# A two-layer graph-attention kernel on one core: keys loaded in four parts, guard scores from step 2, mask rows in 32 pieces, one turn of row maxima, and an output projection in 16-bit halves

## The reference, cut to what matters

```python
# layer 0: h = relu(layernorm(x)); x = x + gat(h, adj)          (8 heads, 4096 nodes, 512 features)
# layer 1: h = relu(layernorm(x))
keys    = einsum('nj,hjk->hnk', h, Wks)      # 8 heads of 64
queries = einsum('nj,hjk->hnk', h, Wqs)
values  = einsum('nj,hjk->hnk', h, Wvs)
adj     = maximum(adj, eye(n))
atts    = einsum('hqk,hmk->hqm', queries, keys) / 64 ** 0.5
atts    = softmax(atts - 1e+16 * (1.0 - adj)[None], axis=-1)
x       = x + einsum('hqm,hmk,hko->qo', atts, values, Wo)
```

## Time and profile before

| | us |
|---|---|
| median of 3 runs | 5021.12 |
| lowest and highest run | 5012.5, 5022.32 |
| the profiled execution, own time | 5012.62 |
| its span, first to last instruction | 5010.9 |
| TensorE matmul busy | 4584.9 (91%) |
| VectorE busy | 3379.6 (67%) |
| ScalarE busy | 3110.1 (62%) |
| GpSimd busy | 3452.4 (69%) |
| mean granted TensorE clock | 0.965 |

### The profile page before, as it was taken

The page is one execution under the profiler, slowest core; times in us unless marked ns, Lnnn a source line. Parts: engine busy times, 40 slices in busy tenths (PEclk is TensorE's granted clock), DMA queues, the critical chain, the costliest instruction groups (busy, mean ns, idle before and its releaser), DMA issues.

```text
span 5010.9 us, 128860 instructions
## 1 busy us (share of the span) xinstructions
PE 4584.9 (91%) x43282; PEld 2220.7 (44%) x43793; DVE 3379.6 (67%) x6969; ACT 3110.1 (62%) x5768; POOL 3452.4 (69%) x2969
## 2 busy tenths in 40 slices
PE   5679999999999878699999899999999999999998
PEld 2322222222222234245555555555555555555555
DVE  6868888888888633556656556557557557466565
ACT  3345555555555333167777677677687687677675
POOL 1157776676777500078878788788788788788786
PEclk8789999999999989789999999999999999999999
DMA  7743233233232234453523425325244334334334
GB/s 310 311 115 97 87 109 93 91 111 93 92 108 70 92 100 118 149 131 91 150 74 110 131 73 139 99 77 156 78 109 134 86 101 135 93 98 130 92 100 120
DMA packets 354936, 583.29 MB, mean 116 GB/s; under 512 B 31200, under 2 KB 219648, under 8 KB 337088
## 3 DMA queue, kind: packets, MB, share of 16 engines
q1 hardware_dynamic: 348992, 557.63, 37.4%
q0 software_dynamic: 5120, 16.78, 1.1%
q10 hardware_dynamic: 128, 0.13, 0.0%
HBM read 497.61 MB, written 76.82 MB: 115 GB/s over the span
## 4 chain that ended last, share of the span: by engine, by line
PE 37%; issue 4%; DMA 3%; SPq 3%; DVE 2%; ACT 1%; POOL 1%; DVEq 0%; ACTq 0%; POOLq 0%
PE d_gd L1475 9%; PE d_sc L1490 6%; PE d_sc L1491 6%; PE d_sc L1492 5%; PE d_acc L1509 3%; PE d_acc L1511 3%; PE d_acc L1519 3%; DMA d_KA<-scratch_kl 3%; PE d_misc L1534 2%; POOL d_PL L1264 1%; SPq L1152 1%; DVE d_junk L1359 1%; ACT d_PH L1305 1%; ACT d_PF L1301 1%; SPq L1153 1%
## 5 line engine op out<-in xcount | busy, mean ns | idle before, releaser
L1264 POOL TENSOR_TENSOR d_PL<-d_PF,d_PH 128x512 f16<-128x512 f32 x2048 | 2357.0, 1176 | 630.6 <-ACT d_PH L1305 628.3
L1359 DVE CUSTOM_DVE_ANT_0 d_junk<-d_gd,d_MR 128x512 bf16<-128x512 f32 x2112 | 1445.0, 690 | 779.2 <-PE d_gd L1475 712.2
L1301 ACT ACTIVATE d_PF<-d_sc 128x512 f32<-128x512 f32 x2048 | 1234.0, 603 | 767.4 <-remote 385.1
L709 DVE SCALAR_TENSOR_TENSOR b_P<-b_R,u,b_A 128x512 f32<-128x512 f32 x1792 | 1202.4, 743 | 217.8 <-ACT b_A L621 154.8
L1305 ACT ACTIVATE d_PH<-d_sc 128x512 f16<-128x512 f32 x2048 | 1239.6, 605 | 0.0
L750 PE MATMUL b_acc<-b_P,V 128*64 128x512 f32 x4096 | 943.2, 601 | 38.1 <-DVE b_P L709 25.3
L1475 PE MATMUL d_gd<-d_KA,d_QA 128*128 128x512 f16 x2112 | 817.7, 387 | 135.6 <-DVE d_gm L1359 47.5
L1490 PE MATMUL d_sc<-d_QA,d_KA 128*128 128x512 f16 x2048 | 783.6, 383 | 64.9 <-ACT d_PH L1305 37.3
L1491 PE MATMUL d_sc<-d_QL,d_KB 128*128 128x512 f16 x2048 | 781.8, 382 | 0.0
L1511 PE MATMUL d_acc<-d_V,d_PH 128*128 128x64 f16 x8192 | 643.4, 194 | 0.0
L1509 PE MATMUL d_acc<-d_V,d_PH 128*128 128x65 f16 x8192 | 642.4, 193 | 0.1
(11 more groups left out here) (128 smaller groups left out, 3916.5 us busy)
## 6 DMA issues: line engine op xcount, KB each, us to landing
d_stage<-in_adj SPq DMA_DIRECT2D x144, 512.0 KB, 4.3
d_V<-scratch_v SPq DMA_DIRECT2D x131, 520.0 KB, 4.3
a_rows<-in_adj SPq DMA_DIRECT2D x32, 2048.0 KB, 9.5
b_stage<-in_adjT SPq DMA_DIRECT2D x128, 512.0 KB, 3.6
d_MT<-scratch_mt SPq DMA_DIRECT2D x36, 1024.0 KB, 6.3
d_KA<-scratch_kh SPq DMA_DIRECT2D x66, 512.0 KB, 8.1
d_KA<-scratch_kl SPq DMA_DIRECT2D x66, 512.0 KB, 10.2
d_KB<-scratch_kh SPq DMA_DIRECT2D x264, 128.0 KB, 3.0
```

The lines of the kernel that those rows point to most:

```text
L709: nc.vector.scalar_tensor_tensor(out=PT[:, m % P_STEPS, h, :], in0=R[:, par, h, :], scalar=T["u"][:, m, h:h + 1], in1=A[m % A_RING][:, :], ...
L1264: eng.tensor_tensor(PL[:, t % H_RING, :], PF[:, t % F_RING, :], PH[:, t % H_RING, :], ALU.subtract).then_inc(s_lowp if by_pool(t) else s_l ...
L1301: nc.scalar.activation(PF[:, t % F_RING, :], sc[t % 2][:, :], ACT.Exp, scale=EXP_SCALE)
L1359: nc.vector.tensor_tensor_reduce(out=junk[:, gi % 2, :], in0=gd[gi % 2][:, :], in1=MR[:, s, c * QB:(c + 1) * QB], scale=1.0, scalar=-3.0e3 ...
```

## The change

In the layer-1 attention:
- `load_ka` loads a quarter of the keys (four loads of 128 KB). It is called at mb = 7, 15, 23 and 31, ahead of `load_kb`, and for the pair *after* the next, into the buffer that the current pair just finished reading. The keys of the first two pairs are loaded before the loop. `load_q` stays at mb = 0.
- Guards run from step 2 instead of 5. A step then has two or three of them, 64 over 27 steps instead of 24.
- The last quarter of the mask tiles is loaded at step 10 of the next block instead of at mb = 31.
- `mask_chunk` works on 32 chunks of 512 columns, from a ring of six, at most steps from 76 to 114.
- `crow` makes the rows of both heads at once: four small matmuls of two rows instead of eight of one. The copy takes two partitions and multiplies by a selector `only`, so that each head keeps its own row.
- wo and oN are kept as high and low 16-bit halves. `project_out` has twelve 16-bit matmuls instead of four 32-bit ones, `copy_turned` two vector instructions instead of one. The halves of wo are made once, before the loop.

```diff
-    CW = 1024
+    CW = 512
-    FIRST_G, LAST_G = 5, 28
+    FIRST_G, LAST_G = 2, 28
+    MT_LATE = 10
-    S_RING = 3
+    S_RING = 6
-    CHUNK_STEPS = [FIRST_C + 5 * ci // 2 for ci in range(CHUNKS)]
+    CHUNK_STEPS = [FIRST_C + 5 * ci // 4 for ci in range(CHUNKS)]
...
-        def load_ka(sp, par, hp):
+        def load_ka(sp, par, hp, i):
+            cols = slice(i * PER * P, (i + 1) * PER * P)
             for x in range(2):
                 row = (2 * hp + x) * D
-                sp.dma_start(KA[0:D, par, x, :], DR["kh"][row:row + D, :]).then_inc(s_KA[par][x], 16)
-                sp.dma_start(KA[D:P, par, x, :], DR["kl"][row:row + D, :]).then_inc(s_KA[par][x], 16)
+                sp.dma_start(KA[0:D, par, x, cols], DR["kh"][row:row + D, cols]).then_inc(s_KA[par][i], 16)
+                sp.dma_start(KA[D:P, par, x, cols], DR["kl"][row:row + D, cols]).then_inc(s_KA[par][i], 16)
...
                             load_q(sp, par, nxt, nb if hp < HP - 1 else (nb + 1) % NB)
-                            load_ka(sp, par, nxt)
                         if mb % PER == PER - 1:
 
                             sp.wait_ge(s_S, nb * TILES + (hp * PAIR + 2 * (mb + 1) + CREDIT))
+                            load_ka(sp, hp % 2, (hp + 2) % HP, mb // PER)
                             load_kb(sp, nxt, mb // PER)
-                            if hp == HP - 1:
+                            if hp == HP - 1 and mb < NT - 1:
                                 load_mt(sp, (nb + 1) % NB, mb // PER)
+                        if step == MT_LATE and not first:
+                            load_mt(sp, nb, GROUPS - 1)
...
             act.wait_ge(s_const, 16 * 2)
-            act.wait_ge(s_set, 5)
+            act.wait_ge(s_set, 6)
+            nc.scalar.activation(woS[:, 0, :, :], xr[:, :, :], ACT.Copy, scale=W_SCALE).then_inc(s_set, 1)
...
+            dve.wait_ge(s_set, 7)
+            nc.vector.scalar_tensor_tensor(out=woS[:, 1, :, :], in0=xr[:, :, :], scalar=W_SCALE, in1=woS[:, 0, :, :],
+                                           op0=ALU.mult, op1=ALU.subtract).then_inc(s_set, 1)
...
-                for x in range(2):
-                    dve.wait_ge(s_crow, it * 2 + (x + 1))
-                    nc.vector.tensor_scalar(QL[D:D + 1, par, x, :], gd[x][D:D + 1, :], shift[D:D + 1, :], None,
-                                            ALU.add).then_inc(s_crowc, 1)
+                dve.wait_ge(s_crow, it + 1)
+                for x in range(2):
+                    nc.vector.tensor_scalar(QL[D:D + 2, par, x, :], gd[0][D:D + 2, :], shift[D:D + 2, :], only[D:D + 2, x:x + 1],
+                                            ALU.add, ALU.mult).then_inc(s_crowc, 1)
...
-                nc.vector.tensor_copy(oN[:, hp, :], misc1[:, :]).then_inc(s_m1, 1)
+                nc.vector.tensor_scalar(oN[:, 0, hp, :], misc1[:, :], O_SCALE, None, ALU.mult).then_inc(s_oNh, 1)
+                dve.wait_ge(s_oNh, nb * HP + (hp + 1))
+                nc.vector.scalar_tensor_tensor(out=oN[:, 1, hp, :], in0=misc1[:, :], scalar=O_SCALE, in1=oN[:, 0, hp, :],
+                                               op0=ALU.mult, op1=ALU.subtract).then_inc(s_m1, 1)
...
                 s, x, c = gi // (2 * MC), gi // MC % 2, gi % MC
-                if s == 0 and c == 0:
-                    if x == 0:
-                        pe.wait_ge(s_Q[par], count * 96 + 96)
-                    pe.wait_ge(s_KA[par][x], count * 32 + 32)
+                if gi == 0:
+                    pe.wait_ge(s_Q[par], count * 96 + 96)
+                if s == 0 and x == 0 and c % (MC // GROUPS) == 0:
+                    pe.wait_ge(s_KA[par][c // (MC // GROUPS)], count * 64 + 64)
...
                 for s in range(SUB):
-                    mm = nc.tensor.matmul(gd[x][D:D + 1, s * P:(s + 1) * P], cmh[:, x, s:s + 1], idh[:, :], start=True, stop=True,
+                    mm = nc.tensor.matmul(gd[0][D:D + 2, s * P:(s + 1) * P], cmh[:, s, :], idh[:, :], start=True, stop=True,
                                           tile_position=(0, D))
...
                 for c in range(HP):
-                    mm = nc.tensor.matmul(misc1[:, :], oN[:, c, s * P:(s + 1) * P], wo[:, c, :],
-                                          start=(c == 0), stop=(c == HP - 1))
+                    for a, b in TERMS:
+                        mm = nc.tensor.matmul(misc1[:, :], oN[:, a, c, s * P:(s + 1) * P], woS[:, b, c, :],
+                                              start=(c == 0 and a == b == 0), stop=(c == HP - 1 and a == 1))
```

More of the change, by code:

```diff
@@ L1032, in layer1_attention @@
     MASK_OPS = 2 + SUB * ROW_OPS
-    FIRST_G, LAST_G = 5, 28
+    FIRST_G, LAST_G = 2, 28
     CROW_STEP = 30
-    S_RING = 3
+    MT_LATE = 10
+    S_RING = 6
     K = D + 1
+    O_SCALE = 16.0
     COPY_STEP, NORM_STEP, TURN_STEP, BACK_STEP, WO_STEP, STORE_STEP = LAG, 3, 5, 7, 11, 28
@@ L1088, in layer1_attention @@
         PL = sb("d_PL", [P, H_RING, QB], F16)
-        oN = sb("d_oN", [P, HP, QB])
-        wo = sb("d_wo", [P, HP, F])
+        oN = sb("d_oN", [P, 2, HP, QB], F16)
+        woS = sb("d_woS", [P, 2, HP, F], F16)
         xr = sb("d_xr", [P, SUB, F])
@@ L1097, in layer1_attention @@
         cm = sb("d_cm", [P, 2, SUB])
-        cmh = sb("d_cmh", [P, 2, SUB], F16)
+        cmh = sb("d_cmh", [P, SUB, 2], F16)
         shift = sb("d_shift", [P, 1])
+        only = sb("d_only", [P, 2])
         idh = sb("d_idh", [P, P], F16)
@@ L1110, in layer1_attention @@
         s_set = sem("constants_set")
-        s_KA = [[sem(f"ka_in{i}{x}") for x in range(2)] for i in range(2)]
+        s_oNh = sem("normalised_high")
+        s_KA = [[sem(f"ka_in{par}{i}") for i in range(GROUPS)] for par in range(2)]
         s_Q = [sem(f"q_in{i}") for i in range(2)]
@@ L1191, in _ @@
                 load_chunk(sp, 0, ci)
-            load_ka(sp, 0, 0)
             load_q(sp, 0, 0, 0)
+            for i in range(GROUPS):
+                load_ka(sp, 0, 0, i)
             for ci in range(S_RING, CHUNKS):
@@ L1197, in _ @@
                 load_chunk(sp, 0, ci)
+            for i in range(GROUPS):
+                load_ka(sp, 1, 1, i)
             for i in range(GROUPS):
@@ L1252, in _ @@
             for par in range(2):
-                for x in range(2):
-                    sp.wait_ge(s_KA[par][x], 32 * (2 * NB + 1 - par))
+                for i in range(GROUPS):
+                    sp.wait_ge(s_KA[par][i], 64 * (2 * NB + 1))
                 sp.wait_ge(s_Q[par], 96 * (2 * NB + 1 - par))
@@ L1258, in _ @@
                 sp.wait_ge(s_V[i], 16 * (HP * NB + (1 if i < GROUPS - 1 else 0)))
-                sp.wait_ge(s_MT[i], 16 * (NB + 1))
+                sp.wait_ge(s_MT[i], 16 * (NB + (1 if i < GROUPS - 1 else 0)))
         def split(eng, engine, nb, t):
@@ L1396, in add_rows @@
                 dve.wait_ge(s_m1w, nb * M1_USES + (HP + s + 2))
-                nc.vector.tensor_tensor(xr[:, s, :], misc1[:, :], xr[:, s, :], ALU.add).then_inc(s_m1, 1)
+                nc.vector.scalar_tensor_tensor(out=xr[:, s, :], in0=misc1[:, :], scalar=1.0 / (O_SCALE * W_SCALE),
+                                               in1=xr[:, s, :], op0=ALU.mult, op1=ALU.add).then_inc(s_m1, 1)
             def finish(nb, hp, mb):
@@ L1414, in _ @@
                 mask_chunk(0, 0, ci)
-                for gi in range(4 * (ci - CH), 4 * (ci - CH) + 4):
+                for gi in range(2 * (ci - CH), 2 * (ci - CH) + 2):
                     if gi >= 0:
                         guard(0, gi, 2 + ROW_OPS * (gi // (2 * MC) + 1) if gi % (2 * MC) == 0 else None)
-            for gi in range(4 * (CHUNKS - CH), GUARDS):
+            for gi in range(2 * (CHUNKS - CH), GUARDS):
                 guard(0, gi, MASK_OPS if gi % (2 * MC) == 0 else None)
@@ L1445, in body @@
                             mask_setup(nb + 1, (nb + 1) % NB)
-                        if step in CHUNK_STEPS:
-                            mask_chunk(nb + 1, (nb + 1) % NB, CHUNK_STEPS.index(step))
+                        for ci in range(CHUNKS):
+                            if step == CHUNK_STEPS[ci]:
+                                mask_chunk(nb + 1, (nb + 1) % NB, ci)
             body(0, True)
@@ L1460, in _ @@
             pe.wait_ge(s_const, 16 * 2)
-            pe.wait_ge(s_set, 5)
+            pe.wait_ge(s_set, 6)
+            pe.wait_ge(s_set, 8)
             pe.sem_inc(s_S, CREDIT)
@@ L1548, in _ @@
                 guard(0, 0, gi, 0)
-            for x in range(2):
-                crow(0, x)
+            crow(0)
             def body(nb, first):
@@ L1558, in body @@
                             pe.wait_ge(s_Q[hp % 2], count * 96 + 96)
-                            for x in range(2):
-                                pe.wait_ge(s_KA[hp % 2][x], count * 32 + 32)
+                            for i in range(GROUPS):
+                                pe.wait_ge(s_KA[hp % 2][i], count * 64 + 64)
                             pe.wait_ge(s_crowc, nb * (2 * HP) + (2 * hp + 2))
@@ L1575, in body @@
                         if mb == CROW_STEP:
```

(3 more changed lines are left out.)

11 lines of the change are left out of this document (6 added, 5 removed).

## The result

| | before | after |
|---|---|---|
| median, us | 5020.63 | 5086.59 |
| lowest, highest | 5012.5, 5022.32 | 5077.2, 5087.38 |
| span of the profiled execution | 5010.9 | 5084.7 |
| mean granted TensorE clock | 0.965 | 0.953 |

What follows compares the result with a forecast made beforehand. TensorE's order of work was taken to bound the layer-1 attention loop. Terms of - 3.7 - 3 - 1.1 - 6.2 + 25 + 1 gave + 12.0 us a block, + 96 in eight, + 3 before the loop; forecast 5116 us, range 5045 to 5165.

Steps and rivals of the forecast that it cites:

- The idling for the queries: TensorE at guard 0 of each pair start, waiting for late query loads: 17.4 us a block, before the clock's loss.
- The queries' wait, within a block: TensorE at guard 0 of the pair starts inside a block: idling of 3.7, 3.7 and 4.7 us.
- The clock: TensorE behind each query wait: clock falls to 1.2 GHz, losing 1.9 us a gap, 7.6 a block.
- The rival that it stays up: TensorE's clock stays at 2.4 GHz behind gaps of 3.7 us, so 60 us go: 5056 us; chance 0.20.
- The jump: TensorE behind the block jump: guard 0 idles for the queries, 4.0 us at one jump, taken as 5.3.
- VectorE: Sixteen more mask pieces and a second copy instruction in the loop: + 1 us a block, between - 5.9 and + 6.
- 0.7 us a pair for the whole spread: Guards over 27 steps fill TensorE's holes in steps 2 to 4: saves about 3 us a block.
- Projection: Output projection on TensorE: twelve 16-bit matmuls save 0.93 us a row group, 3.7 a block.
- The turn of maxima: Small matmuls on TensorE, four instead of eight: saves 0.27 us a turn, 1.1 a block.
- The keys' wait: TensorE's waits for keys vanish with keys loaded a pair ahead: 6.2 us a block saved, clock included.
- the faster rival: SyncE's issues cost under about 0.25 us, so queries come in time: 4912 us; chance 0.08.
- The lock on the shared port: VectorE's 16 added mask pieces each wait for GpSimd again: 0.41 us each, or up to 0.75.

Runs made afterwards that it cites:

- experiment 1: The changed kernel with the six query loads issued ahead of the four key loads; 4913.74 us, ratio to before 0.9787.
- experiment 2: The changed kernel with guards from step 5 instead of 2; 4943.73 us, ratio to before 0.9844.
- experiment 3: The changed kernel with 16 useless 512-column matmuls on TensorE ahead of guard 0's wait for the queries; 5038.11 us, ratio to before 1.0038.
- Experiment 6: The changed kernel with the last quarter of the mask tiles loaded at mb = 31 again, ahead of the block jump; 5112.98 us, ratio to before 1.0186.
- experiment 5: The changed kernel with query loads ahead of key loads and the mask rows in 16 pieces of 1024 columns; 4913.07 us, ratio to before 0.9793.
- experiment 10: The changed kernel with query loads first, guards from step 3 and 16 mask pieces of 1024 columns; 4905.99 us, ratio to before 0.9792.
- experiment 8: The changed kernel with query loads first and guards from step 3; 4904.25 us, ratio to before 0.9774.
- experiment 7: The kernel before with only the output projection in 16-bit halves, including two instructions in copy_turned; 4997.54 us, ratio to before 0.9957.
- experiment 4: The changed kernel with the mask rows in 16 pieces of 1024 columns and a ring of three again; 5063.86 us, ratio to before 1.0087.
- experiment 9: Query loads first, guards from step 3, plus the last quarter of KA and KB loaded behind the block jump; 4903.51 us, ratio to before 0.9787.

## Why the prediction was right, and which terms were mis-sized

The sign and its cause were right, and the size came out within the range in part by luck, since errors offset each other. The idling for the queries is the example. The forecast's terms make 139 us in eight blocks, and 135.3 were measured. But behind the six jumps it was 12.4 where the terms make 31.8, and at the other 26 pair starts 122.9 where they make 107.4; the sum in the prediction counted eight jumps, and there are six. The first two blocks have none ahead of them. By the end of block 1 the changed kernel was 24 us behind (forecast 15), nearly half of it by the end of the first wait, of 9.3 us; block 2 added 12, as forecast; the six blocks behind a jump added 6.5 each instead of 12. Step by step:

- **The queries' wait, within a block: right.** Forecast 3.7, 3.7 and 4.7 us of idling; the pair starts of one block show 3.86, 4.46 and 5.55, and blocks 3 to 7 on average 3.9, 4.5 and 5.1. Steps 2 and 3 of these three pairs grew by 20.5 us a block, where idling and clock were forecast at 17.8. The last query issue came 7.1 us behind the first issue, as worked out. Experiments 1 and 2 take the wait away by two independent ways and give back 173 and 143 us.
- **The clock: right.** I charged 1.9 us a gap, 60 in all. Filling the gaps gave 48 net, and the mean clocks put the whole at about 70 (experiment 3). The rival that it stays up fell: 0.50 behind the gap.
- **The jump: wrong.** The term "I take 5.3" for the wait behind the block jump measured 1.5 to 3.1, mean 2.1. I took the mask-tile load out of the sum with its issue time of 1.35 us alone. Experiment 6 put it back and got 5.15 us of waiting and 26 us of run time. With its clock term the forecast was 7.2 us a jump, and steps 2 and 3 there grew by 2.9: 26 us too much in six jumps. The next error is of the same size; block 1 and the starts of the other pairs, which cost more than forecast, offset part of both.
- **VectorE: wrong in sign.** I took + 1 us a block. From the step lengths, what waits for VectorE in pairs 3 and 4 (steps 6 to 29, against the same steps of pair 2) went from 5.3 us a block to 2.8, so the term is - 2.5, within the - 5.9 to + 6 that I allowed. The extra work was there (8.2 us a block for pieces, 2.8 for the copy) but hidden (experiments 5 and 10); what I left out is that guards over 27 steps instead of 24 ease VectorE as much as TensorE. Experiments 2 and 8 bear it out: from step 5 to step 3 is worth 39 us, where 0.7 us a pair for the whole spread makes 22, and step 8, where the copy is felt, falls from 3.28 to 2.68 in pairs 1 to 3. Their other difference, the place of the query loads, adds no wait in either. The size of the pieces matters less: with guards from 5 the same steps lose 3.7 us a block with small pieces (experiment 2) and 4.6 with large ones (experiment 7); with guards from 2 it is 2.8 with small and 2.4 with large ones (experiment 4).
- **TensorE's own way over the jump: not in the forecast.** Step 0 behind a jump went from 7.3 to 8.5 us (blocks 3 to 7). The cause stays open (experiment 9).
- **Projection: right on TensorE** (0.92 us less for a row group, forecast 0.93), with a cost on VectorE in the old spread that the new spread hides (experiment 7).
- **The turn of maxima:** step 30 fell from 3.06 to 2.84 us, 0.22 against 0.27.
- **The keys' wait:** gone, as said. Steps 5 and 6, where it stood, are 6.2 us a block shorter, though each step 5 has a guard more; forecast was 6.2.
- **Issue time, the faster rival:** refuted by the issue rows, 0.5 to 0.65 us each, and by experiment 1. The page "DMA: Bandwidth & Descriptors" of the Trainium skill, section "Issuing engines are not separate DMA queues", calls the issue time usually small relative to the transfer; here twelve issues in a row took 7.7 us, and the last landed 2.4 us after its issue.
- **The lock on the shared port:** a 512-column piece took 0.87 us in the loop, against 0.48 alone before it: the 0.39 beside GpSimd are nearly the 0.46 of a 1024-column piece (1.21 against 0.75), so what is waited for hardly shrinks with the piece. The page "SBUF — State Buffer" of the Trainium skill, section "Who interferes with whom", states that VectorE in a two-port mode and GpSimd lock each other out for a whole instruction; these numbers agree, though no trace shows the mode. It did not reach the time.

## What to carry to other kernels

Before moving a consumer earlier, list everything that it waits for, and where each stands in its issuing queue; here the keys were brought forward and the queries, which the same instruction needs, went behind them. The order of issues on a DMA queue is a resource like an engine: twelve issues at 0.6 us (7.7 in all) last longer than a query load takes to land (2.4), so the load that is wanted first goes first. And when a part of a change looks bad or good in a run with one large stall, try it again with the stall removed: the small mask pieces cost 23 us with it and nothing that can be measured without.

## What the runs showed of the hardware that I had not expected

- A 1 MB load issued just ahead of a loop's jump lengthened SyncE's own way over the jump from 3.6 to 5.7 us; 768 KB of smaller loads ahead of it did not lengthen TensorE's.
- The same jump took SyncE 0.7 us in the kernel with large mask pieces (experiment 4), with the same loads ahead of it.
- Idling of 3.9 us on TensorE was followed by 3.3 us and more at 1.2 GHz, though the clock was still at 2.4 GHz during the idle itself. Sixteen matmuls without use, 3.6 us, kept it up at most pair starts; of four where 2.0 to 2.3 us of idling followed them, the clock held at one (3495.1) and fell to 0.50 at three (3855.2, 4215.5, 4936.8).
